# Key and value rows multiplied by their learning rates on GpSimd as they land, and three plain token products on VectorE

## The reference

```python
gate = ki @ w0_
hb = ki @ w2_
sg = silu(gate)
hidden = sg * hb
dhidden = vi @ w1_.transpose(0, 2, 1)
dhbm = dhidden * sg
dgba = silu_backprop(dhidden * hb, gate)
w1g = newtonschulz5(einsum('bch,bcd->bhd', hidden * lr1i, vi))
w0g = newtonschulz5(einsum('bcd,bch->bdh', ki * lr0i, dgba))
w2g = newtonschulz5(einsum('bcd,bch->bdh', ki * lr2i, dhbm))
w1_, w0_, w2_ = w1_ + w1g, w0_ + w0g, w2_ + w2g    # then each is brought back to its first column norms
oi = silu(qi @ w0_) * (qi @ w2_) @ w1_
```

## Time and profile before

| | |
|---|---|
| median of 3 runs | 1683.79 us (1683.41 to 1691.88) |
| profiled execution, first to last instruction | 1633.0 us |
| TensorE matmuls busy | 1477.8 us, 90% |
| VectorE busy | 1275.3 us, 78% |
| ScalarE busy | 1004.9 us, 62% |
| GpSimd busy | 788.0 us, 48% |

### The profile page before, as it was taken

How to read it: one execution, slowest core, us unless ns; L and a number is a source line. 1 busy time by engine, 2 the same in 40 slices (tenths; PEclk the granted TensorE clock), 3 DMA queues, 4 the chain that set the end, 5 groups by cost and what they waited for, 6 DMA issues and landing times. The chain is left out here.

```text
span 1633.0 us, 44257 instructions
## 1 busy us (share of the span) xinstructions
PE 1477.8 (90%) x12478; PEld 987.5 (60%) x12543; DVE 1275.3 (78%) x4523; ACT 1004.9 (62%) x2284; POOL 788.0 (48%) x837
## 2 busy tenths in 40 slices
PE   7995899999999999999985399999999999999996
PEld 4664677777777777776764255555555555555774
DVE  4663678888888888888886687777777777774998
ACT  4773577666777676777663166666666666663221
POOL 1332234666766666666667434443434443443333
PEclk9996899999999999999997599999999999999998
DMA  3875454445555543223322466766677676633996
GB/s 117 259 234 158 133 155 132 145 135 157 180 164 167 156 144 90 84 85 99 99 69 104 153 189 201 216 201 198 207 201 204 196 210 195 205 89 78 260 259 152
DMA packets 264982, 264.39 MB, mean 162 GB/s; under 512 B 87467, under 2 KB 236313, under 8 KB 264752
## 3 DMA queue, kind: packets, MB, share of 16 engines
q1 hardware_dynamic: 204464, 176.51, 37.4%
q0 software_dynamic: 19968, 51.16, 8.6%
q10 hardware_dynamic: 40320, 33.96, 8.5%
HBM read 142.70 MB, written 122.98 MB: 163 GB/s over the span
## 5 line engine op out<-in xcount | busy, mean ns | idle before, releaser
L1736 POOL DMA_INDIRECT scratch_y<-eo,goes x224 | 225.4, 1006 | 338.6 <-ACT eo L1830 297.1
L1761 PE MATMUL e_psGU<-wexp,e_xT 128*64 x896 | 290.5, 467 | 0.2 <-issue 0.2
L1763 PE MATMUL e_psGU<-e_up,e_xT 128*64 128x352 f32 x896 | 290.5, 467 | 0.0
L1378 POOL TENSOR_TENSOR f_wnr<-f_wss,f_half 128x4 f32<-128x4 f32 x96 | 112.3, 1169 | 197.3 <-DVE f_wss L1201 197.2
L1368 POOL DMA_INDIRECT scratch_buf<-rows,dest x180 | 183.3, 1018 | 44.0 <-issue 44.0
L1851 ACT ACTIVATE e_up<-wexp 128x704 f32 x224 | 177.1, 790 | 20.4 <-POOLq L1726 20.2
L1761 PEld LDWEIGHTS e_psGU<-wexp,e_xT 128*64 128x64 f32 x896 | 113.7, 137 | 122.0 <-issue 122.0
L1971 DVE COPY e_down<-wexp 128x512 f32 x224 | 93.9, 419 | 94.2 <-PE e_psD L1786 92.8
L1830 ACT ACTIVATE eo<-e_psD 128x256 f32<-128x256 f32 x224 | 85.5, 384 | 95.2 <-PE e_psD L1786 47.7
L1819 ACT ACTIVATE e_sgm<-e_psGU 128x176 f32<-128x176 f32 x224 | 71.2, 318 | 77.7 <-PE e_psGU L1763 60.8
L1780 PE MATMUL e_psD<-wexp,e_hT 112*64 x448 | 115.2, 379 | 1.6 <-DVE e_hT L1926 1.6
(11 more groups left out here) (335 smaller groups left out, 4362.1 us busy)
## 6 DMA issues: line engine op xcount, KB each, us to landing
e_xg<-scratch_buf ACTq DMA_DIRECT2D x436, 66.0 KB
scratch_y<-f_blank SPq DMA_DIRECT2D x64, 384.0 KB
c_g<-scratch_y SPq DMA_DIRECT2D x64, 384.0 KB, 9.5
scratch_qkvT<-q_tT SPq DMA_DIRECT2D x16, 768.0 KB, 5.1
wexp<-in_wgT SPq DMA_DIRECT2D x64, 176.0 KB
wexp<-in_wuT SPq DMA_DIRECT2D x64, 176.0 KB
scratch_buf<-f_blank SPq DMA_DIRECT2D x65, 132.0 KB, 1.9
scratch_kv<-q_y SPq DMA_DIRECT2D x16, 512.0 KB, 2.8
```

The source lines that it names most:

```text
L1378: pool.tensor_tensor(wnr[:, x, cols], wss[:, x, cols], half[:, 0:Q], ALU.pow).then_inc(wn1[x].sem, 1)
L1736: pool.indirect_dma_start(out=T["y"], out_offset=bass.IndirectOffsetOnAxis(goes[:, n:n + 1], 0), in_=eo[:, n % OB, :], in_offset=None, bou ...
L1761: pe.matmul(psGU[0:RT, n % 2, 0:2 * F], xT[:, n % 4, k, 0:RT], ring[:, bass.ds(at[n] + k * 2 * F, 2 * F)], start=(k == 0), stop=(k == KD - 1))
L1763: mm = pe.matmul(psGU[RT:P, n % 2, 0:2 * F], xT[:, n % 4, k, RT:P], up2[:, n % 2, k * 2 * F:(k + 1) * 2 * F], start=(k == 0), stop=(k == K ...
```

## The change

The three rates are no longer multiplied into `pp`, `dhb` and `hid`, but into the other operand of each gradient. A new step `rate` on GpSimd waits for an item's loads, makes `klr2`, the key rows times the third rate, and then multiplies the key rows by the first and the value rows by the second rate in place. `grads_0` waits for it. VectorE's three steps are one plain 128x256 product each and don't wait for the loads. To make room for `klr2`, `A2` becomes the same memory as `sq`.

```diff
 POOL_ORDER = (
-    ("row_root", 0, 1, 1), ("root", 1, 1), ("root_x", 1, 3), ("row_root", 0, 1, 2), ("send", 0, 0, 0),
+    ("row_root", 0, 1, 1), ("root", 1, 1), ("root_x", 1, 3), ("rate", 1, 0), ("row_root", 0, 1, 2), ("send", 0, 0, 0),
     ("renorm", 0, 1), ("send", 0, 0, 1), ("row_root", 1, 1, 0), ("root_o", 1, 2), ("send", 0, 0, 2),
-    ("row_root", 1, 1, 1), ("root", 0, 0), ("root_x", 0, 2), ("row_root", 1, 1, 2), ("send", 1, 0, 0),
+    ("row_root", 1, 1, 1), ("root", 0, 0), ("root_x", 0, 2), ("rate", 0, -1), ("row_root", 1, 1, 2), ("send", 1, 0, 0),
...
+        klr2 = sb("klr2", [P, 2, D])
...
+        A2 = sq
...
-                lhsT, rhs = {W1: (hid[rows, x, cols], vv), W2: (kk, dhb[rows, x, cols]), W0: (kk, dg[rows, x, cols])}[m]
+                lhsT, rhs = {W1: (hid[rows, x, cols], vv), W2: (klr2[rows, x, cols], dhb[rows, x, cols]),
+                             W0: (kk, dg[rows, x, cols])}[m]
...
             def grads_0(x, it):
+                pe.wait_ge(rated[x].sem, rated[x].at(it, 2))
                 pe.wait_ge(dgd[x].sem, dgd[x].at(it, 1))
...
             def both(x, it):
-                v.wait_ge(k_in[x].sem, k_in[x].at(it, 8))
                 v.wait_ge(td[x].sem, td[x].at(it, 1))
                 v.wait_ge(u2d[x].sem, u2d[x].at(it, 1))
-                scaled(pp, x, prod[:, x, W2, 0:D], 0, us).then_inc(ppd[x].sem, 1)
+                v.tensor_tensor(pp[:, x, :], prod[:, x, W2, 0:D], us[:, x, :], ALU.mult).then_inc(ppd[x].sem, 1)
...
+            def rate(x, it):
+                pool.wait_ge(k_in[x].sem, k_in[x].at(it, 8))
+                if it:
+                    pool.wait_ge(gps[x].sem, gps[x].at(it - 1, LOTS))
...
+                pool.tensor_tensor(by_head(klr2, 0, H), by_head(kv, 0, H), rates(2 * H, H), ALU.mult).then_inc(rated[x].sem, 1)
+                pool.wait_ge(rated[x].sem, rated[x].at(it, 1))
+                pool.tensor_tensor(by_head(kv, 0, 2 * H), by_head(kv, 0, 2 * H), rates(0, 2 * H), ALU.mult).then_inc(rated[x].sem, 1)
+
+            rate(0, 0)
             pool.wait_ge(initn, 3)
```

More of the change, by code:

```diff
@@ L575, in phase_fast_weights @@
         lr = sb("lr", [P, 2, NLR])
+        klr2 = sb("klr2", [P, 2, D])
         s, sg, us, hid, dhb, pp, dg = (sb(n, [P, 2, D]) for n in ("s", "sg", "us", "hid", "dhb", "pp", "dg"))
-        X, XT, sq, A, Bm, X2, X2T, A2, B2 = (sb(n, [P, 2, LOTS, Q, P], BF16) for n in (
-            "X", "XT", "sq", "A", "Bm", "X2", "X2T", "A2", "B2"))
+        X, XT, sq, A, Bm, X2, X2T, B2 = (sb(n, [P, 2, LOTS, Q, P], BF16) for n in (
+            "X", "XT", "sq", "A", "Bm", "X2", "X2T", "B2"))
+        A2 = sq
         wsq = sb("wsq", [P, 2, LOTS, Q, P])
@@ L611, in phase_fast_weights @@
         q_in = sig("q_in", 2, 16)
+        rated = sig("rated", 2)
         tg, td, tb = (sig(n, 1) for n in ("tg", "td", "tb"))
@@ L1114, in first_tables @@
                 v.tensor_scalar(code[:, :, 7], code[:, :, 7], later[:, 0:1], None, ALU.add).then_inc(w_scaled, 1)
[L1116 to L1123, removed]
             def gate(x, it):
@@ L1149, in token_dhb @@
             def token_dhb(x, it):
-                v.wait_ge(k_in[x].sem, k_in[x].at(it, 8))
                 v.wait_ge(td[x].sem, td[x].at(it, 1))
                 v.wait_ge(sgd[x].sem, sgd[x].at(it, 1))
-                scaled(dhb, x, prod[:, x, W2, 0:D], 2, sg).then_inc(dhbd[x].sem, 1)
+                v.tensor_tensor(dhb[:, x, :], prod[:, x, W2, 0:D], sg[:, x, :], ALU.mult).then_inc(dhbd[x].sem, 1)
             def token_hid(x, it):
-                v.wait_ge(k_in[x].sem, k_in[x].at(it, 8))
                 v.wait_ge(tb[x].sem, tb[x].at(it, 1))
                 v.wait_ge(sgd[x].sem, sgd[x].at(it, 1))
-                scaled(hid, x, prod[:, x, W1, 0:D], 1, sg).then_inc(hidd[x].sem, 1)
+                v.tensor_tensor(hid[:, x, :], prod[:, x, W1, 0:D], sg[:, x, :], ALU.mult).then_inc(hidd[x].sem, 1)
                 if it == 0:
@@ L1334, in _, with by_head, rates @@
                       allow_small_or_imprecise_dtypes=True).then_inc(tables, 1)
+            def rate(x, it):
+                pool.wait_ge(k_in[x].sem, k_in[x].at(it, 8))
+                if it:
+                    pool.wait_ge(gps[x].sem, gps[x].at(it - 1, LOTS))
+                def by_head(a, lo, n):
+                    return a[:, x, lo * HD:(lo + n) * HD].rearrange("p (j d) -> p j d", d=HD)
+                def rates(lo, n):
+                    return lr[:, x, lo:lo + n].unsqueeze(2).broadcast_to([P, n, HD])
+                pool.tensor_tensor(by_head(klr2, 0, H), by_head(kv, 0, H), rates(2 * H, H), ALU.mult).then_inc(rated[x].sem, 1)
+                pool.wait_ge(rated[x].sem, rated[x].at(it, 1))
+                pool.tensor_tensor(by_head(kv, 0, 2 * H), by_head(kv, 0, 2 * H), rates(0, 2 * H), ALU.mult).then_inc(rated[x].sem, 1)
+            rate(0, 0)
             pool.wait_ge(initn, 3)
@@ L1389, in _ @@
             in_order(POOL_ORDER, {
-                "root_o": root_o, "root_x": root_x, "send": send,"root": root, "row_root": row_root, "renorm": renorm})
+                "rate": rate, "root_o": root_o, "root_x": root_x, "send": send,"root": root, "row_root": row_root, "renorm": renorm})
     return rows_out
```

## The result

The changed kernel is slower. In the first comparison it took 1754.68 us in the median (1750.78 to 1760.21), the kernel before 1686.85 us, a ratio of 1.0405 (1.0375 to 1.0435). In a second one, on another chip, it took 1724.43 us beside 1633.06 us, a ratio of 1.0554 (1.0518 to 1.0589).

A forecast was written before the change was run, and what follows sets the result against it. TensorE is full behind `hidden_back`, so its delay counts: 23 x 2.54 + 5 x 2.45 = 70.7 us, plus 0.5 at the start. Span 1633.0 + 71 = 1704, plus 50.8 around it: 1755 us, range 1729 to 1790.

The forecast's parts named there:

- The terms of the lateness: GpSimd's `row_root`: landing 2.4 us plus products 1.7 make it 3.04 late; less 0.5 slack, `hidden_back` 2.54 late per half.
- rival 6: TensorE pauses 2.5 us per half; should its granted clock fall, the time is over 1800 us; chance 0.03.
- The time around the span: Outside the traced span: 1683.79 - 1633.0 = 50.8 us, if the profiled execution was like the median run.
- Rival 1 and 2: 1: loads in time, GpSimd's work hidden, 1684 us, chance 0.05. 2: also VectorE's relief counts, 1666 us, chance 0.02.
- 0.5 us of slack: Between the end of W1's renorm and `hidden_back`: 0.6 us, less 0.1 for a signal.
- Rival 4 and 5: 4: landing takes 3.5 us, 1786 us, chance 0.12. 5: TensorE's small waits or quicker landing give back, 1730 to 1741, 0.13.
- Rival 3, the port: SBUF port shared by GpSimd and VectorE holds GpSimd's products 0.44 us per half, 12 us: 1767 us; chance 0.15.
- the branch that the prediction named first: At the shared port VectorE's `place` instructions are held, and nothing is lost since VectorE waits at `factors` anyway.

The follow-up runs named there:

- the wait alone: Kernel before, plus GpSimd waiting for the same eight loads at the place of `rate` and writing one number per partition; 1706.95 us, ratio 1.0081.
- the work alone: Kernel before, plus two GpSimd products of the same sizes on its own buffers at that place, no outside wait; 1702.03 us, ratio 1.0055.
- the plain products: Changed kernel without `rate`: VectorE's three plain products stay, gradients use bare rows, so the output differs; 1694.06 us, ratio 1.0014 to the kernel before.

## Why the prediction was right, and where its sum was not

*The mechanism* was right in each step that it names: GpSimd waits for the loads just issued, `row_root` and the renorm of W1 queue behind, `hidden_back` starts 0.1 us after the renorm, `read` and with it the next loads are late by as much, in 28 halves. Putting the step behind the renorm or the loads ahead takes nearly all of it away; the wait alone and the work alone give 0.8 and 0.5%.

*The terms of the lateness.* In the half shown the last `lr` is issued 4.95 us after `load_q`. From there to `klr2` it takes 2.25 us (490.39 - 488.14), taken as 2.4. The two products and the signal between them take 1.69 us (490.39 to 492.08), taken as 1.7. From `row_root` to the renorm it is 2.32 us, taken as 2.63: the renorm had waited for VectorE's `factors` and now finds them done. That makes this half 1.97 us late. Others are later, since SyncE issues their last `lr` up to 6.4 us after `load_q` (5.2 in the mean) and one landing took 3.8 us. The mean is 2.27 us per half instead of 2.5, 63.5 us instead of 70.7.

*The clock* was rival 6, with a chance of 0.03, since no row showed it, and at over 1800 us. It is real but smaller: 35 us, a third of the price, in the execution shown. What failed is the sum, which took the time behind a pause of 2.5 us as unchanged. The trace at hand could have warned: behind the gap of 11.38 us at the phase's start the granted clock is 0.73 in the mean from 145 to 206 us, and I had not asked what a shorter gap does.

*The time around the span*, 50.8 us, does not exist; it is 1.7 us. From the quicker chip's trace, 1633 + 1.7 + 71 = 1706 us was the right reading, and 1724 us was measured there: an error of 18 us in the sum. The 71 us were added to a time of the slower kind of chip for a wrong reason, but it was the right base, because the changed kernel was measured on that kind too.

*That 1755 us meets 1754.68 so closely is in part luck.* The difference of the medians is 67.8 us (1754.68 - 1686.85). No trace of the kernel before was taken there, but that of the plain products, from a chip with like times and at 1.0014 of the kernel before, can stand for it. Beside it the changed kernel's first profile has `hidden_back` 12.61 us after `load_q` instead of 10.38, which is 62 us in 28 halves where 71 were forecast. The way from `hidden_back` to the next `load_q` adds only 2 us, 13.22 us against 13.14, although the granted clock falls here too (0.95 in the mean of the phase). In most halves that keep the full clock this way is shorter than without the `rate` step, as in these two:

```profile
491.93:505.69 13.76, 11.65 (x120) 9.42 (x120) 9.48 (x27) 8.97 (x22) 9.14 (x10) 1.00 0.47 159
...
867.56:880.24 12.68, 11.95 (x119) 9.47 (x120) 9.64 (x27) 7.43 (x15) 9.70 (x10) 1.00 0.15 55
```

The first row is of the plain products, the second of the changed kernel. So on this chip the clock's price, which the sum lacks, was offset by shorter pauses elsewhere, which it lacks too. Why they get shorter stays open.

*Rival 1 and 2*, the loads in time and a gain from VectorE, are refuted. Rival 1's condition was also worked out too narrowly: with a landing in no time and 0.5 us of slack, a last load issued before 517.5 would have been early enough, not 517.1. The plain products are 0.42 us each, as forecast, and give nothing (1.0014). *Rival 4 and 5*: the way from issue to `klr2` is 2.3 us in the median, and TensorE's waits for `X2T` are as before (10.9 us over the phase), so neither decided.

*Rival 3, the port.* The lock is there and costs nothing, by the branch that the prediction named first. VectorE's `place` beside GpSimd's two products, in the half shown above:

```profile
490.57 0.52 DVE L1277 SCALAR_TENSOR_TENSOR key<-f_lz,f_ebase 128x64 f32<-128x64 f32 x1
491.12 1.09 DVE L1280 TENSOR_TENSOR key<-key,mask 128x64 f32<-128x64 f32 x1
492.24 0.23 DVE L1282 MAX8 keys<-key 128x8 f32<-128x64 f32 x1
...
493.13 0.17 DVE L1199 SCALAR_TENSOR_TENSOR f_wnr<-f_wnr,f_wn0i 128x4 f32<-128x4 f32 x1 [0.38 <-POOL f_wnr L1387]
```

Instructions of 0.22 and 0.23 us take 0.52 and 1.09 us, each until GpSimd's product is over; GpSimd's own run at 0.61 and 1.04 us. (The 0.22 and 0.23 us are those of the same two instructions in the kernel before.) The Trainium skill (SBUF — State Buffer, "SBUF: two separate sides") says that the one that starts first keeps the shared ports to its end; by that rule, the trace agrees. VectorE still waits 0.38 us for GpSimd at `factors`.

## What to carry to other kernels

Work that fits into an engine's idle time is hidden only if what it waits for is there when that idle time begins: ask when the data is issued, not when it is first used, and what is queued behind the waiting instruction. If a queue's transfers are themselves released by the step that now waits for them, the delay closes a loop and is paid in every round. And price a new pause of TensorE twice, once for its length and once for the clock behind it.

## What the runs showed that I had not expected

- The 28 pauses of TensorE before `hidden_back` were 0.8 to 3.4 us long, in a stream that is otherwise full. Behind 15 of them, of 1.8 to 3.4 us, the granted clock fell from 1.00 to 0.50. The pause's length alone does not sort them: one of 2.82 us went free, one of 1.81 us did not.
- The same program takes 1632 us on three chips and 1687 to 1692 us in the first comparison and on a fourth chip (medians). On that slower one, in the version with the plain products alone, TensorE stands 0.87 us before `project` for a reason that the trace does not name, and ScalarE 1.81 us with its input done:

```profile
519.89 1.10 PE L952 MATMUL spare<-wproj,f_onT 128*128 128x256 f32 x4 [0.87 <-issue]
```

What causes this was not found.
